# A decoder layer on one core: four tiles for the second residual, two score pairs for the last batch's softmax, the convolution's products in a step of their own, and a new order of all engines

## The reference

```python
x = x + _L0_attn_ref(_layernorm(x, axis=-1), ...)                # linear attention, 16 heads of 8
x = x + _L0_xattn_ref(_layernorm(x, axis=-1), ctx_1024, ...)     # causal softmax attention on ctx
x = x + _L0_ffn_ref(_layernorm(x, axis=-1), ...)                 # 8 experts, top 2, plus a convolution
```

## Time and profile before

| | us |
|---|---|
| median of three runs | 196.93 (196.34 to 197.08) |
| the profiled execution, its time | 196.06 |
| its span, first to last instruction | 194.3 |
| PE busy | 166.0 |
| DVE busy | 163.4 |
| ACT busy | 124.9 |
| POOL busy | 113.8 |

### The profile page before, as it was taken

How to read it: one execution, slowest core, us unless ns; L and a number is a source line. 1 busy time by engine, 2 the same in 40 slices (tenths; PEclk the granted TensorE clock), 3 DMA queues, 4 the chain that set the end, 5 groups by cost and what they waited for, 6 DMA issues and landing times.

```text
span 194.3 us, 5501 instructions
## 1 busy us (share of the span) xinstructions
PE 166.0 (85%) x1812; PEld 114.5 (59%) x1812; DVE 163.4 (84%) x458; ACT 124.9 (64%) x281; POOL 113.8 (59%) x204
## 2 busy tenths in 40 slices
PE   6958697778898899995999999988988998797973
PEld 6846484545566556672866576656646546554542
DVE  6665878847787889998999989999999799399893
ACT  2036563528857798785776398858976568756560
POOL 7864877951932873798236633657366167754432
PEclk9999999969999999999999999999999999999999
DMA  5931131120332210013203211232121000000001
GB/s 174 321 142 41 36 84 48 46 69 15 97 83 57 59 32 21 1 46 107 71 4 83 60 48 31 55 86 57 44 59 33 27 7 2 27 3 0 30 2 54
DMA packets 17796, 11.00 MB, mean 57 GB/s; under 512 B 2388, under 2 KB 17108, under 8 KB 17768
## 3 DMA queue, kind: packets, MB, share of 16 engines
q1 hardware_dynamic: 17768, 10.66, 18.7%
HBM read 3.10 MB, written 1.05 MB: 21 GB/s over the span
## 4 chain that ended last, share of the span: by engine, by line
DVE 29%; PE 23%; issue 21%; POOL 18%; ACT 6%; DVEq 1%; POOLq 0%; ACTq 0%
DVE negmax L839 7%; PE max_pair L966 4%; POOL rstd L488 4%; POOL xn L498 4%; PE ffn_bank L966 4%; PE self_bank L966 4%; PE pv_bank L966 4%; DVE convT L944 3%; ACT probs L641 3%; POOL probs L524 2%; DVE stats L735 2%; PE soft_pair L966 2%; POOL hid L533 2%; POOL vareps L480 1%; POOL xres L506 1%
## 5 line engine op out<-in xcount | busy, mean ns | idle before, releaser
L839 DVE TENSOR_REDUCE negmax<-max_pair 128x4 f32<-128x1024 f32 (+1 forms) x48 | 58.5, 1218 | 6.6 <-PE max_pair L966 6.1
L641 ACT ACTIVATE probs<-soft_pair 128x1024 f32<-128x1024 f32 x48 | 49.0, 1020 | 8.8 <-PE soft_pair L966 8.8
L524 POOL TENSOR_SCALAR_AFFINE_SELECT probs<-probs 128x512 f32<-128x512 f32 (+1 forms) x48 | 37.5, 795 | 21.8 <-ACT probs L641 21.8
L966 PE MATMUL pv_bank<-probs,vs 128*32 128x128 f32 (+1 forms) x512 | 23.7, 328 | 1.6 <-POOL probs L524 1.4
L966 PEld LDWEIGHTS pv_bank<-probs,vs 128*32 128x32 f32 x512 | 14.4, 109 | 10.6 <-POOL probs L524 3.7
L966 PE MATMUL soft_pair<-qs,ks 64*128 64x256 bf16 (+1 forms) x256 | 18.9, 247 | 1.1 <-ACT probs L641 1.0
L966 PE MATMUL max_pair<-causal,picks 64*128 64x128 bf16 (+1 forms) x192 | 15.5, 240 | 4.8 <-DVE negmax L839 3.2
L606 ACT ACTIVATE xn<-x,shift,rstd 128x128 f32<-128x128 f32 x32 | 14.0, 488 | 8.4 <-DVE shift L759 8.4
L966 PE MATMUL max_pair<-ks,qs 64*128 64x128 bf16 (+1 forms) x256 | 18.8, 245 | 0.0
L488 POOL TENSOR_TENSOR rstd<-vareps,exponent 128x2 f32<-128x2 f32 x24 | 17.4, 725 | 2.0
L533 POOL TENSOR_TENSOR hid<-hraw,cw 128x256 f32<-128x256 f32 x16 | 10.3, 649 | 13.6 <-DVE hraw L921 7.1
(11 more groups left out here) (195 smaller groups left out, 386.8 us busy)
## 6 DMA issues: line engine op xcount, KB each, us to landing
ks<-kparts SPq DMA_DIRECT2D x48, 64.0 KB, 2.0
qs<-qparts SPq DMA_DIRECT2D x48, 64.0 KB, 2.1
out_dram<-result SPq DMA_DIRECT2D x8, 128.0 KB, 1.8
loaded<-packed_dram SPq DMA_DIRECT2D x1, 768.0 KB, 7.7
loaded<-packed_dram SPq DMA_DIRECT2D x1, 640.0 KB, 8.8
qs<-maxparts SPq DMA_DIRECT2D x32, 4.0 KB
loaded<-packed_dram SPq DMA_DIRECT2D x1, 462.5 KB, 6.3
loaded<-packed_dram SPq DMA_DIRECT2D x2, 192.0 KB, 3.0
```

The lines of the kernel that those rows point to most:

```text
L524: nc.gpsimd.affine_select(out=v, in_=v, compare_op=ALU.is_ge, fill=0.0, base=0, pattern=[[0, n], [1, P]], channel_multiplier=-1).then_inc( ...
L641: nc.scalar.activation(probs[b.par][g][:, k, :], soft_pair[:, :], ACT.Exp).then_inc(exp_done, 1)
L839: nc.vector.tensor_reduce(maxima, max_pair[:, :].rearrange("p (u h k) -> p u h k", u=2, h=n), AX.X, ALU.max, negate=True).then_inc(max_rea ...
L966: return nc.tensor.matmul(out, lhsT, rhs, start=start, stop=stop, skip_group_check=True)
```

## The change

- x2, the tile of the second residual, has four buffers, taken by c % 4, where it had two. `residual2` waits for skip and norm3 of batch c-4 instead of c-2. norm3 on ACT gets a wait for relu7 of batch c-2.
- For the last batch, units 3 and 5 of the soft scores go to max_pair, the others stay on soft_pair. Unit 3 waits for all reads of max_pair, units 4 and 5 for the exp two units before, not one. Batch 7's ffn_gate_up, whose banks are in max_pair, waits for the last exp instead of the last read of the maxima.
- The convolution's products leave ffn_down for a step ffn_conv of their own on PE; it waits for the taps, and for hidT in batches 0 to 5 or for the second hraw in batches 6 and 7.
- All five lists of ORDER are new; they hold the same steps and ffn_conv.

The lists, cut to the stretches that matter here:

```diff
    "sp": """
-        load.0.0 load.0.1 load.0.2 load.0.3 load.0.4 load.0.5 load.0.6 load.0.7 hi_k.0.0 mid_k.0.0 lo_k.0.0
...
+        load.0.0 load.0.1 load.0.2 load.0.3 load.0.4 load.0.5 load.0.6 load.0.7 lo_k.0.0 mid_k.0.0 hi_k.0.0
+        hi_q.0.0 lo_q.0.0 mid_q.0.0 hi_k.1.0 mid_k.1.0 hi_q.1.0 send_max.0.0 mid_q.1.0 lo_k.1.0 lo_q.1.0
...
    "pool": """
-        routes.0.0 picks.0.0 ones.0.0 ones.0.1 heads.0.0 rstd1.0.0 clear_v.0.0 clear_v.0.1 bias.0.0 rstd1.1.0
...
-        sig.0.0 mask.1.5 bias.5.0 bias.6.0 mask.2.0 mask.2.1 mask.2.2 rstd1.7.0 norm1.6.0 mask.2.3 mask.2.4
-        hid.0.0 hid.0.1 norm1.7.0 rstd2.5.0 rstd3.1.0 mask.2.5 lo_k.4.0 lo_k.5.0 lo_q.4.0 base.0.0 mask.3.0
-        mask.3.1 mask.3.2 rstd3.2.0 sig.1.0 lo_q.5.0 mask.3.3 mask.3.4 mask.3.5 hid.1.0 hid.1.1 rstd2.6.0
...
+        causal.0.0 rstd1.0.0 ones.0.0 ones.0.1 clear_v.0.0 heads.0.0 clear_v.0.1 rstd1.1.0 rstd1.2.0 norm1.2.0
+        bias.0.0 picks.0.0 lo_k.0.0 rstd1.3.0 rstd2.0.0 norm1.3.0 routes.0.0 lo_q.0.0 bias.1.0 bias.2.0 bias.3.0
+        rstd2.1.0 rstd2.2.0 clear_v.0.2 clear_v.0.3 bias.4.0 lo_k.1.0 rstd1.4.0 rbias.0.0 lo_q.1.0 norm1.4.0
...
+        bias.6.0 lo_k.4.0 sig.0.0 mask.2.0 rstd1.6.0 rstd1.7.0 norm1.6.0 norm1.7.0 mask.2.1 mask.2.2 mask.2.3
+        mask.2.4 lo_q.4.0 mask.2.5 hid.0.0 hid.0.1 rstd2.5.0 rstd3.1.0 base.0.0 lo_q.5.0 lo_k.5.0 mask.3.0
...
    "act": """
-        outT.6.0 max_hi.7.1 exp.7.1 hidT.4.0 exp.7.2 norm3.5.0 exp.7.3 x3T.5.0 o2T.6.0 exp.7.4 tanh_r.5.0
-        exp.7.5 tanh_g.5.0 tap.5.0 outT.7.0 norm3.6.0 relu7.5.0 tanh_g.5.1 x3T.6.0 tap.6.0 o2T.7.0 hidT.5.0
...
+        tanh_r.4.0 exp.6.4 max_hi.7.0 tanh_g.4.0 exp.6.5 tanh_g.4.1 exp.7.0 relu7.4.0 outT.6.0 max_hi.7.1
+        exp.7.1 hidT.4.0 exp.7.2 norm3.5.0 o2T.6.0 exp.7.3 x3T.5.0 exp.7.4 tanh_r.5.0 exp.7.5 tap.5.0 tanh_g.5.0
+        outT.7.0 relu7.5.0 norm3.6.0 tanh_g.5.1 o2T.7.0 x3T.6.0 tanh_r.6.0 tap.6.0 hidT.5.0 tanh_g.6.0 norm3.7.0
...
    "dve": """
-        var1.1.0 stats1.2.0 phi_q.0.0 var1.2.0 phi_k.0.0 norm1.1.0 kvsum.0.0 div1.0.0 div1.0.1 div1.0.2
-        rest_k.0.0 phi_q.1.0 phi_q.2.0 x1.0.0 stats2.0.0 var2.0.0 phi_k.1.0 stats1.3.0 var1.3.0 shift2.0.0
...
-        rest_k.1.0 kvsum.3.0 stats2.2.0 reduce.0.0 div1.3.0 div1.3.1 var2.2.0 reduce.0.1 div1.3.2 shift2.2.0
-        rest_q.1.0 reduce.0.2 max_mid.0.0 x1.3.0 rest_k.2.0 reduce.0.3 stats2.3.0 reduce.0.4 var2.3.0 reduce.0.5
-        stats1.6.0 max_mid.0.1 phi_q.4.0 rest_q.2.0 reduce.1.0 phi_k.4.0 reduce.1.1 kvsum.4.0 reduce.1.2
-        div1.4.0 shift2.3.0 div1.4.1 max_mid.1.0 var1.6.0 rest_k.3.0 reduce.1.3 div1.4.2 reduce.1.4 div2.0.0
-        div2.0.1 reduce.1.5 max_mid.1.1 rest_q.3.0 x2.0.0 x1.4.0 reduce.2.0 stats3.0.0 var3.0.0 reduce.2.1
-        shift3.0.0 stats2.4.0 var2.4.0 reduce.2.2 rest_k.4.0 max_mid.2.0 stats1.7.0 phi_q.5.0 route.0.0
-        shift2.4.0 route.0.1 reduce.2.3 route.0.2 reduce.2.4 gate.0.0 phi_k.5.0 reduce.2.5 kvsum.5.0
...
-        stats3.4.0 rest_q.7.0 reduce.6.4 gate.3.1 tap.3.1 var3.4.0 times_up.3.1 reduce.6.5 tap.3.2 tap.3.3
-        max_mid.6.1 skip.3.0 skip.3.1 reduce.7.0 div2.5.0 div2.5.1 shift3.4.0 finish.3.0 reduce.7.1 reduce.7.2
-        route.4.0 max_mid.7.0 x2.5.0 route.4.1 route.4.2 reduce.7.3 route.4.3 gate.4.0 route.4.4 times_up.4.0
-        route.4.5 reduce.7.4 stats3.5.0 route.4.6 gate.4.1 reduce.7.5 times_up.4.1 tap.4.1 var3.5.0 max_mid.7.1
-        skip.4.0 tap.4.2 tap.4.3 div2.6.0 skip.4.1 div2.6.1 shift3.5.0 finish.4.0 x2.6.0 route.5.0 route.5.1
-        stats3.6.0 route.5.2 route.5.3 route.5.4 gate.5.0 route.5.5 var3.6.0 tap.5.1 times_up.5.0 tap.5.2
...
+        stats1.2.0 phi_k.0.0 var1.2.0 rest_k.0.0 phi_q.0.0 kvsum.0.0 norm1.1.0 div1.0.0 div1.0.1 div1.0.2
+        stats1.3.0 var1.3.0 x1.0.0 stats2.0.0 var2.0.0 stats1.4.0 phi_k.1.0 shift2.0.0 phi_k.2.0 kvsum.1.0
+        phi_q.1.0 phi_q.2.0 kvsum.2.0 div1.1.0 div1.1.1 div1.1.2 rest_q.0.0 div1.2.0 div1.2.1 var1.4.0 div1.2.2
+        stats1.5.0 clear.0.5 x1.1.0 stats2.1.0 x1.2.0 var2.1.0 var1.5.0 stats2.2.0 stats1.6.0 phi_k.3.0
+        shift2.1.0 rest_k.1.0 var2.2.0 reduce.0.0 phi_q.3.0 kvsum.3.0 reduce.0.1 div1.3.0 rest_q.1.0 reduce.0.2
+        div1.3.1 div1.3.2 max_mid.0.0 shift2.2.0 rest_k.2.0 reduce.0.3 reduce.0.4 x1.3.0 reduce.0.5 max_mid.0.1
+        stats2.3.0 var2.3.0 reduce.1.0 rest_q.2.0 reduce.1.1 shift2.3.0 phi_k.4.0 reduce.1.2 rest_k.3.0 var1.6.0
+        stats1.7.0 max_mid.1.0 phi_q.4.0 kvsum.4.0 reduce.1.3 div1.4.0 div1.4.1 reduce.1.4 div1.4.2 reduce.1.5
+        div2.0.0 div2.0.1 max_mid.1.1 rest_q.3.0 reduce.2.0 x2.0.0 stats3.0.0 x1.4.0 var3.0.0 reduce.2.1
+        shift3.0.0 reduce.2.2 phi_q.5.0 stats2.4.0 max_mid.2.0 rest_k.4.0 var2.4.0 route.0.0 reduce.2.3
...
+        rest_q.7.0 route.3.6 gate.3.1 reduce.6.4 times_up.3.1 tap.3.2 var3.4.0 reduce.6.5 skip.3.0 tap.3.3
+        shift3.4.0 max_mid.6.1 skip.3.1 div2.5.0 reduce.7.0 div2.5.1 finish.3.0 reduce.7.1 x2.5.0 reduce.7.2
+        route.4.0 stats3.5.0 route.4.1 var3.5.0 max_mid.7.0 route.4.2 route.4.3 gate.4.0 reduce.7.3 times_up.4.0
+        route.4.4 route.4.5 reduce.7.4 shift3.5.0 gate.4.1 route.4.6 reduce.7.5 times_up.4.1 tap.4.1 max_mid.7.1
+        tap.4.2 skip.4.0 tap.4.3 skip.4.1 div2.6.0 div2.6.1 finish.4.0 x2.6.0 stats3.6.0 route.5.0 route.5.1
+        route.5.2 route.5.3 route.5.4 tap.5.1 route.5.5 var3.6.0 tap.5.2 gate.5.0 route.5.6 times_up.5.0
+        shift3.6.0 skip.5.0 skip.5.1 div2.7.0 div2.7.1 tap.5.3 gate.5.1 times_up.5.1 x2.7.0 stats3.7.0 route.6.0
...
    "pe": """
-        self_x_t.0.0 self_q1.0.0 cross_k_v.0.0 self_kv.0.0 self_sum.0.0 self_x_t.1.0 self_x_t.2.0 self_out.0.0
-        self_q1.1.0 self_q1.2.0 self_o_t.0.0 self_kv.1.0 self_proj.0.0 self_kv.2.0 self_sum.1.0 self_out.1.0
...
-        self_out.3.0 max.0.1 cross_q2.1.0 max.0.2 self_o_t.3.0 cross_k_v.2.0 maxrow.0.0 self_proj.3.0 max.0.3
-        cross_norm_t.2.0 self_x_t.4.0 max.0.4 cross_q2.2.0 self_q1.4.0 soft.0.0 max.0.5 soft.0.1 maxrow.0.1
-        self_kv.4.0 max.1.0 soft.0.2 cross_k_v.3.0 max.1.1 soft.0.3 self_sum.4.0 soft.0.4 max.1.2 self_out.4.0
...
-        ffn_gate_up.4.0 max.7.3 soft.6.5 pv.6.0 max.7.4 ffn_gate_up.4.1 soft.7.0 max.7.5 pv.6.1 maxrow.7.1
-        soft.7.1 ffn_hid_t.4.0 out_t.6.0 soft.7.2 ffn_down.4.0 soft.7.3 o2_t.6.0 ffn_x_t.5.0 soft.7.4
-        ffn_router.5.0 o_proj.6.0 soft.7.5 ffn_gate_up.5.0 pv.7.0 pv.7.1 ffn_gate_up.5.1 out_t.7.0 ffn_x_t.6.0
...
+        self_x_t.0.0 self_q1.0.0 cross_k_v.0.0 self_kv.0.0 self_sum.0.0 self_out.0.0 self_x_t.1.0 self_x_t.2.0
+        self_o_t.0.0 self_q1.1.0 self_q1.2.0 self_proj.0.0 self_kv.1.0 self_kv.2.0 self_sum.1.0 self_sum.2.0
...
+        self_o_t.2.0 self_proj.1.0 self_proj.2.0 self_kv.3.0 cross_k_v.1.0 max.0.0 self_sum.3.0 cross_norm_t.1.0
+        max.0.1 cross_q2.1.0 self_out.3.0 max.0.2 cross_k_v.2.0 maxrow.0.0 max.0.3 self_o_t.3.0 max.0.4
+        self_proj.3.0 cross_norm_t.2.0 soft.0.0 max.0.5 self_x_t.4.0 soft.0.1 maxrow.0.1 self_q1.4.0
+        cross_q2.2.0 max.1.0 soft.0.2 self_kv.4.0 max.1.1 soft.0.3 cross_k_v.3.0 max.1.2 soft.0.4 pv.0.0
...
+        ffn_x_t.4.0 o_proj.5.0 max.7.2 ffn_router.4.0 soft.6.4 maxrow.7.0 ffn_gate_up.4.0 soft.6.5 max.7.3
+        pv.6.0 max.7.4 ffn_gate_up.4.1 soft.7.0 max.7.5 pv.6.1 maxrow.7.1 soft.7.1 ffn_hid_t.4.0 out_t.6.0
+        soft.7.2 ffn_conv.4.0 ffn_down.4.0 o2_t.6.0 soft.7.3 soft.7.4 ffn_x_t.5.0 o_proj.6.0 soft.7.5
+        ffn_router.5.0 pv.7.0 ffn_gate_up.5.0 pv.7.1 out_t.7.0 ffn_gate_up.5.1 o2_t.7.0 ffn_x_t.6.0 o_proj.7.0
...
+        ffn_router.6.0 ffn_hid_t.5.0 ffn_gate_up.6.0 ffn_conv.5.0 ffn_down.5.0 ffn_gate_up.6.1 ffn_x_t.7.0
+        ffn_router.7.0 ffn_gate_up.7.0 ffn_gate_up.7.1 ffn_hid_t.6.0 ffn_conv.6.0 ffn_down.6.0 ffn_hid_t.7.0
+        ffn_conv.7.0 ffn_down.7.0
...
```

The rest of the diff, with a line of context:

```diff
@@ -254,3 +254,3 @@
 
-        x2 = two("x2_", [P, T, C])
+        x2 = [sb(f"x2_{i}", [P, T, C]) for i in range(4)]
         x3T = two("x3T", [C, KC - 1 + S])
@@ -351,2 +351,6 @@
 
+        def pair_of_soft(b, u):
+
+            return max_pair if b.c == B - 1 and u in (3, 5) else soft_pair
+
         @block.sync
@@ -603,3 +607,4 @@
                             act.wait_ge(skip_done, b.count(2, -2))
-                    source = {2: x1[b.c % 4], 3: x2[b.par]}[n]
+                            act.wait_ge(relu7_done, b.count(2, -2))
+                    source = {2: x1[b.c % 4], 3: x2[b.c % 4]}[n]
                     for i in range(T):
@@ -640,3 +645,3 @@
                     act.wait_ge(pe_pv, b.count(2, g - 3))
-                nc.scalar.activation(probs[b.par][g][:, k, :], soft_pair[:, :], ACT.Exp).then_inc(exp_done, 1)
+                nc.scalar.activation(probs[b.par][g][:, k, :], pair_of_soft(b, u)[:, :], ACT.Exp).then_inc(exp_done, 1)
 
@@ -721,3 +726,3 @@
             def source(n, b):
-                return {1: x_of(b), 2: x1[b.c % 4], 3: x2[b.par]}[n]
+                return {1: x_of(b), 2: x1[b.c % 4], 3: x2[b.c % 4]}[n]
 
@@ -866,6 +871,6 @@
                 dve.wait_ge(pe_o, b.count(1, 1))
-                if b.since(2):
```

(34 more changed lines are left out.)

156 lines of the change are left out of this document (73 added, 83 removed).

## The result

The changed kernel takes 189.14 us (median, 188.99 to 189.28) beside 196.63 of the kernel before: a ratio of 0.9635, 95% interval 0.9574 to 0.9695. The forecast was 194.3, its range began at 191.5; so the sign was right and the gain, 7.5 us, was almost three times what the sum had. The profiled executions give 194.3 and 187.5 us of span: 6.8. Ratios and their intervals leave out executions over 1.5% longer than the fastest of the same kernel (two of five in e2, three of ten in e5, three of four in e10, one each in e7 and e16); medians and ranges hold all.

A forecast was written before the change was run, and what follows sets the result against it. The prediction took DVE, busy 163.4 of 194.3 us, as the bound and priced changes in its idle time: -0.9-1.7-0.8+0.8+0 = -2.6, off the median of 196.93, gave 194.3 us; range 191.5 to 198.6.

The forecast's parts named there:

- start and batch 0: From the start through batch 0's score reductions: earlier self_out.0 and sixth reduction take DVE idle time away, -0.9 (0 to -2.0).
- batch 1's hand-offs: DVE idle between batch 1's score reductions, where work between falls short of the shortest turn: 1.34 us old, 0.46 new.
- third norm: Batch 1: DVE's wait of 0.78 for rstd3.1 goes as POOL does both norm1 earlier, -0.8 (0 to -2.6).
- DVE beside POOL: DVE's two-input instructions stretched beside POOL: no reason the new order favours either, 0 (-3 to +4.6).
- tail: Last stretch: x2.6 earlier but its idle time moves to route.5.0, with new short places, +0.8 (-1.2 to +1.5).
- the outer end: Start and batch 0's bound of -2.0: PE's clock does not fall, half of 3.5 us go, over half on the path.
- Hand-offs of the other batches: DVE idle between score reductions outside batches 0 and 1; the hand-off term for all later batches was -1.7 (0 to -3.2).
- rival (b): Idle time only moves: if PE paces the reductions, filled hand-offs become waits elsewhere, 196.8 us; chance 0.19.
- Rival (a): The tail opens: second pair and earlier o2T make its term -1.2, in all -4.6, 192.3 us; chance 0.22.
- The edits of code: Four x2 tiles, added norm3 wait and convolution step, without the order: 0 each, the convolution step at most 0.1.
- The prediction's own signs: Wrong if DVE's busy time moves over 2 us, or the last exp ends 1 us earlier against the last max_mid.
- rival (c): Slower, DVE beside POOL: new neighbours stretch more two-input instructions, +4.6-2.6=+2.0, 198.9 us; chance 0.17.

The follow-up runs named there:

- e2: The kernel before's code (two x2 tiles, one score pair, convolution's products inside ffn_down) with the five new lists: ratio 0.9743 to the kernel before.
- e5: The kernel before with batch 4's first steps in batch 0 moved to their new places on PE and ACT: 197.03 us, ratio 1.0005.
- e10: The changed kernel with 12 unread matmuls at its start instead of 18: 188.76 us.
- e7: The kernel before with one POOL step moved, norm1 of batch 7 behind rstd3.1 instead of two places ahead: 197.49 us, ratio 1.0038.
- e16: e5 with self_kv.4 moved too and unread matmuls on PE, five in batch 0 and three in the tail: 195.17 us, ratio 0.9943.
- e14: The kernel before with unread matmuls where PE stalls, eight in batch 0 and three in the tail: 194.52 us, ratio 0.9894.
- e1: The changed kernel's code with the five old lists, ffn_conv directly ahead of each ffn_down: ratio 1.0002 to the kernel before.
- e8: The kernel before with POOL's masks cut to each unit's first 128x128 block: 192.27 us, ratio 0.9825.
- e9: The changed kernel with POOL's masks cut to each unit's first 128x128 block: 187.76 us, ratio 0.9573 to the kernel before.
- e3: The changed kernel with all soft scores on one pair and the old waits: ratio 0.9742 to the kernel before.
- e4: The changed kernel with the convolution's products back inside ffn_down, behind hidT: ratio 0.9618 to the kernel before.
- e15: The changed kernel with 12 unread matmuls at its start instead of 18, the other six in PE's next gaps: 186.82 us, ratio 0.9505.

## Why the prediction fell short

DVE's busy and idle time between three marks, us (idle counted from DVE's first instruction, 1.07; e14 is the kernel before with its clock kept):

| up to the end of | before: busy, idle | e14: busy, idle | after: busy, idle |
|---|---|---|---|
| max_mid.1.1 (at 60.69, 59.16, 57.48) | 43.8, 15.8 | 43.7, 14.4 | 44.0, 12.5 |
| the last max_mid (162.95, 161.41, 157.95) | 95.7, 6.6 | 95.7, 6.6 | 93.8, 6.7 |
| the last finish (192.03, 190.47, 185.23) | 24.0, 5.1 | 24.0, 5.1 | 22.4, 4.9 |

Of the 6.8 us of span, 1.5 are the clock, 3.3 busy time and 2.0 idle time (the profiled execution of before has one fall and lies at the upper end of its group, hence 1.5 and not 1.1). Beside the prediction's sum, the clock as before to e14 and the rest of the idle time as e14 to after:

| term | predicted | measured |
|---|---|---|
| start and batch 0, idle | -0.9 | -0.5 |
| batch 1's hand-offs, idle | -0.9 | -1.4 |
| clock | 0 | -1.5 |
| other hand-offs and third norm, idle | -1.6 | +0.1 |
| DVE beside POOL, all busy time | 0 | -3.3 |
| tail, idle | +0.8 | -0.2 |
| sum | -2.6 | -6.8 |

The busy time named under the third norm and the tail below is part of the -3.3. Term by term:

- **Start and batch 0, -0.9, and batch 1's share of the hand-offs, 1.34 to 0.46.** Right together, -1.8 against -1.9, by luck in the parts: the start, with its first reduction 0.7 earlier, gave 0.2 (rstd1.3 ahead of rstd2.0), and batch 1's hand-offs more than walked. The clock came on top, -1.5. The prediction had it as the outer end and put nothing of it into the sum, though the lists that it walked through took away the stall of 1.19 (the longest left in 36 to 44 is 0.96). e5 and e1 show that this stall alone doesn't decide it.
- **Hand-offs of the other batches, the rest of -1.7.** Wrong in sum. The idle time ahead of reductions and max_mids is 9.7 before, 8.3 in e14, 8.5 after. Batches 1 and 7 fell (2.5 to 1.5 as walked, 1.2 to 0.7, less than the walked 0.9); batches 3 and 6 rose from 0 and 0.3 to 1.3 each, of which the walk saw nothing. It went by DVE's own list and by one shortest turn, and missed the other queues. In batch 3, 0.92 is the DMA of lo_q.3 behind batch 4's k on SP, where the prediction priced moved DMAs at 0. In batch 6, 0.56 is max_mid.6.1 waiting for ACT, whose new list has outT.5 (0.57) ahead of max_hi.6.1. Most of the rest, 0.35 at reduce.3.5 and 0.54 at reduce.6.0, is waits for PE's scores, as rival (b) put it for the middle; DVE's busy time fell by 1.0 and 2.0 in these batches, so it may only come to these waits earlier; this wasn't tested.
- **The third norm, -0.8.** The wait of 0.78 went, but DVE has 0.92 more idle time at reduce.3.0, ahead of it in the same batch. Its outer end, the stretch behind it, is what was gained: the shift and the two instructions behind it lost some 1.8 over their medians, both halves of skip.0.1 together got 0.6 longer, and the busy time up to max_mid.3.1 in that batch fell by 1.0. e7 shows that even this is no property of the one move.
- **DVE beside POOL, 0.** The step that failed most: "I see no reason that it favours either, so I take 0". It was -3.3 by the busy time, at the bound of -3. The durations' part, 2.2, is which instructions meet a mask (e8, e9): in the kernel before eight instructions end with a mask's end and are 4.2 us over their medians together, in the changed one seven, 1.8 over. The prediction's 6.1 us had taps and shifts alone; of these fifteen instructions seven are shifts, the other eight steps of route, which it hadn't counted. It could have been walked like the waits, since the lists say which mask stands near which shift.
- **The tail, +0.8.** Wrong in sign: -1.8, of which busy time gives 1.6 (o ended 2.16 after the last max_mid, not 2.85 as walked). Rival (a), with -1.2, had the mechanism right, as x2.6 and the last exps came earlier, but not its price in idle time. That is only 0.2, because two effects nearly cancel: with one pair (e3) the new order makes the idle time behind the last max_mid 2.0 longer, and the second pair takes 2.2 away. The prediction sized the pair at "at most 0.6 on ACT", by ACT's own waits in the old order; it is the PE steps queued behind the soft scores that it frees.
- **The edits of code, 0.** Right for the tiles, the added wait and the convolution's step (e1, e4).

The prediction's own signs told this: busy time moved by more than 2, and the last exp ended 1.27 earlier against the last max_mid. The range failed since its low end took in little more than rival (a), -4.6, while the clock's part of the start's outer end and the ports' outer end came true together. (Its upper end, 198.6, leaves out rival (c)'s own time, 198.9, though the text says that it takes in most of (c).)

What stays open: why the old order met more masks was counted, not made by an experiment that moves DVE's steps alone; 0.65 us between e16 and e14 are explained only by the wait shown, and their unread matmuls stand at different places; and when a stall of PE brings a fall of the clock.

## What to carry to other kernels

Price a stall of PE with the clock that it may lose behind it, and read the clock of several executions beside their times before any list is judged. Walk the queues that feed the engine, DMA issues too, and not its own list alone. Price a second buffer by what is queued behind the instruction that it frees, in the order that the change will have, and not by that instruction's wait in the old one. Where one engine's instructions differ several times in length beside another's, walk their neighbours through the new lists; "no reason either way" is no zero.

## What the runs showed of the hardware

- One fall of TensorE's clock costs the kernel before some 1.1 us of span (medians of 192.9, 193.9 and 195.1 at a mean clock of 1.00, 0.991 and 0.982 to 0.983), and with eleven unread matmuls in the gaps no execution had one (e14: four at 1.00, 194.3 to 194.9 us).
- Where a fall lies differs between kernels and between executions: 40.5 to 44 us before, some 2 us later in e5, in the first 20 us in e10, 36 to 40.5 in e15, and in e1, whose lists are the old ones and whose stall of 1.17 is still there, only in the tail.
- With the masks cut to one block, POOL's busy time falls by 24 us and DVE's by 6.0, though DVE has the same instructions.
